# Value weights of a banded attention kernel: 16 contiguous elements a head, or 128 columns that stand 16 elements apart

## What is computed

```python
x = x + attention(layernorm(x), Wq, Wk, Wv, Wo)   # 16 heads of 16, a window of 64 keys back
x = x + ffn(layernorm(x), W1, b1, W2, b2)         # 1024 wide, relu, W1 and W2 rounded to -1, 0, 1
```

## Time and profile before

| | |
|---|---|
| time, median of 3 runs | 694.15 us (693.81 to 694.34) |
| profiled execution, its span | 690.4 us |
| profiled execution, its own time | not listed apart; the median is 3.75 us over the span |
| PE busy | 649.0 us, 94% of the span |
| DVE busy | 628.3 us, 91% |
| ACT busy | 623.9 us, 90% |
| POOL busy | 618.0 us, 90% |
| DMA packets | 497988 for 61.17 MB |

### The profile page before, as it was taken

How to read it: one execution, slowest core, us unless ns; L and a number is a source line. 1 busy time by engine, 2 the same in 40 slices (tenths; PEclk the granted TensorE clock), 3 DMA queues, 4 the chain that set the end, 5 groups by cost and what they waited for, 6 DMA issues and landing times.

```text
span 690.4 us, 24485 instructions
## 1 busy us (share of the span) xinstructions
PE 649.0 (94%) x8048; PEld 552.7 (80%) x8048; DVE 628.3 (91%) x1596; ACT 623.9 (90%) x2649; POOL 618.0 (90%) x869
## 2 busy tenths in 40 slices
PE   7668699999999999999999999999999999998887
PEld 5446488888888888888888888887888888887776
DVE  5779889999999999999999999999999999899864
ACT  5689899999999999999999999998999999898833
POOL 7388999999999999999999999999899999999930
PEclk9879989999999999999999999999999999999999
DMA  8576656465756656475756657475665646464000
GB/s 293 80 98 103 75 96 73 77 86 74 125 73 99 98 99 95 77 95 72 128 68 101 96 92 105 51 117 74 102 91 99 74 82 71 61 93 70 18 31 31
DMA packets 497988, 61.17 MB, mean 89 GB/s; under 512 B 470724, under 2 KB 493510, under 8 KB 497864
## 3 DMA queue, kind: packets, MB, share of 16 engines
q1 hardware_dynamic: 487160, 50.82, 51.2%
q10 hardware_dynamic: 10704, 8.80, 4.2%
HBM read 11.86 MB, written 8.39 MB: 29 GB/s over the span
## 4 chain that ended last, share of the span: by engine, by line
PE 40%; POOL 32%; issue 10%; ACT 9%; DVE 6%; DMA 1%; SPq 0%; POOLq 0%; DVEq 0%; ACTq 0%
POOL p L393 13%; POOL tl L417 10%; PE ps L1089 9%; PE ps L1077 7%; ACT p L496 6%; PE ps L987 5%; POOL th L411 5%; PE ps L967 5%; PE ps L1024 4%; PE ps L1035 3%; PE ps L1050 3%; ACT hTh L573 1%; PE ps L1062 1%; POOL rstdC L386 1%; PE ps L960 1%
## 5 line engine op out<-in xcount | busy, mean ns | idle before, releaser
L496 ACT ACTIVATE p<-ps,negm 128x96 f32<-128x96 f32 x1024 | 340.3, 375 | 8.4 <-DVE negm L711 7.7
L417 POOL TENSOR_TENSOR tl<-pt,th 128x384 f16<-128x384 f32 x256 | 234.6, 916 | 16.3 <-ACT th L505 1.8
L496 ACT ACTIVATION_READ_ACCUMULATOR p<-ps,negm 128x1 f32 x1024 | 248.5, 244 | 0.0
L393 POOL TENSOR_TENSOR p<-p,rden 128x384 f32<-128x384 f32 x256 | 214.3, 837 | 7.3 <-DVE rden L718 6.9
L724 DVE STREAM_TRANSPOSE pt<-p 128x384 f32<-128x384 f32 x256 | 141.5, 553 | 14.3 <-POOL p L393 12.9
L711 DVE TENSOR_REDUCE negm<-ps 128x4 f32<-128x384 f32 x256 | 136.0, 531 | 10.4 <-PE ps L967 8.1
L967 PE MATMUL ps<-k,qbd 128*128 128x96 f16 x1536 | 125.2, 208 | 0.0
L967 PEld LDWEIGHTS ps<-k,qbd 128*128 128x128 f16 x1536 | 106.0, 99 | 9.6
L987 PE MATMUL ps<-th,vb 128*128 128x96 f16 (+1 forms) x1120 | 97.1, 202 | 1.8 <-POOL tl L417 1.8
L1077 PE MATMUL ps<-xTCh,w1T 128*128 128x256 f16 x512 | 97.6, 272 | 0.8 <-ACT xTCh L568 0.8
L573 ACT ACTIVATE hTh<-ps 128x512 f16<-128x512 f32 x128 | 79.6, 623 | 19.9 <-PE ps L1077 19.7
(11 more groups left out here) (139 smaller groups left out, 1486.7 us busy)
## 6 DMA issues: line engine op xcount, KB each, us to landing
k<-kst SPq DMA_DIRECT2D x32, 288.0 KB, 4.1
vb<-vd SPq DMA_DIRECT2D x256, 32.0 KB, 2.6
out<-x SPq DMA_DIRECT2D x32, 256.0 KB, 2.5
qbd<-qs SPq DMA_DIRECT2D x254, 32.0 KB, 2.3
x<-in_L_attn_hidden ACTq DMA_DIRECT2D x15, 512.0 KB, 5.4
kw<-kst SPq DMA_DIRECT2D x31, 192.0 KB, 3.8
k<-kst SPq DMA_DIRECT2D x31, 144.0 KB, 3.4
vb<-in_L_ffn_W SPq DMA_DIRECT2D x2, 1024.0 KB, 7.6
```

The costliest lines, as they stand in the source:

```text
L393: e.tensor_tensor(p3, p3, rden[n % 4][:, :].unsqueeze(2).to_broadcast([128, 4, 96]), ALU.mult).then_inc(s_nm, 1)
L417: e.tensor_tensor(tl[g % 2][:, o], pt[n % 3][:, :], th[g % 2][:, o], ALU.subtract).then_inc(s_lo, 1)
L496: ins = e.activation(p[:, 96 * u:96 * u + 96], bank[:, 96 * u:96 * u + 96], ACT.Exp, bias=m[:, u:u + 1], accum_out=r[:, u:u + 1])
```

## The change

`vd` and `vb` get another order of dims. The innermost two are now t and g, and d stands outside them: `vd` is `[128, v 2, h 4, d 16, t 4, g 4]`, and `vb` has one more dim for m ahead of v. So for one head and one part v the values (d t g) are one run of 256 elements, 512 bytes, and a DMA of `place_v` moves two runs a partition where it moved 32. The weight columns (v h d) of a key block now stand 16 elements (32 bytes) apart. ACT and DVE write `vd` through the new order: 8 rows of 64 elements as before, but the 64 stand 16 elements apart, and DVE reads the high half with that step too. The sizes of the buffers, the bytes, the counts of instructions on all engines, their order and their semaphores are the same.

```diff
-        vd = sb("vd", [128, 4, 4, 2, 4, 16], f16)
-        vb = [sb(f"vb{i}", [128, 4, 4, 4, 2, 4, 16], f16) for i in range(3)]
+        vd = sb("vd", [128, 2, 4, 16, 4, 4], f16)
+        vb = [sb(f"vb{i}", [128, 4, 2, 4, 16, 4, 4], f16) for i in range(3)]
...
-                    src = vd[32 * m:32 * m + 32, :, :, :, h, :].rearrange("p t g v d -> p (t g v) d")
-                    dst = vb[b][32 * h:32 * h + 32, m, :, :, :, h, :].rearrange("p t g v d -> p (t g v) d")
+                    src = vd[32 * m:32 * m + 32, :, h].rearrange("p v d t g -> p v (d t g)")
+                    dst = vb[b][32 * h:32 * h + 32, m, :, h].rearrange("p v d t g -> p v (d t g)")
...
-                e.activation(vd[:, 2 * u:2 * u + 2, :, 0].rearrange("p t g h d -> p (t g) (h d)"),
+                e.activation(vd[:, 0, :, :, 2 * u:2 * u + 2, :].rearrange("p h d t g -> p (t g) (h d)"),
...
-                hi, lo = (vd[:, 2 * u:2 * u + 2, :, v].rearrange("p t g h d -> p (t g) (h d)") for v in range(2))
+                hi, lo = (vd[:, v, :, :, 2 * u:2 * u + 2, :].rearrange("p h d t g -> p (t g) (h d)") for v in range(2))
...
-                    lhs = vb[(c if k >= 0 else c - 1) % 3][:, k % 4, k % 16 // 4, g].rearrange("p v h d -> p (v h d)")
+                    lhs = vb[(c if k >= 0 else c - 1) % 3][:, k % 4, :, :, :, k % 16 // 4, g].rearrange("p v h d -> p (v h d)")
```

## The result

The changed kernel takes 768.67 us (median; 767.07 to 768.79) against 694.25 us: a ratio of 1.1059, with a 95% interval of 1.1041 to 1.1077. That is 74.4 us slower, outside the range of 692 to 750.

The account below looks back on a forecast made before the run. PE and POOL were taken to bound the kernel in turns, with four engines nearly full. Span 690.4 + 0 (DMAs) + 0 (loads) + 1.3 (writes) = 691.7 us, plus 3.75 to the median, 695.4 us; range 692 to 750.

Parts of the forecast that it names:

- PE and POOL in turns, four engines nearly full: Whole kernel: the chain is PE for 40% and POOL for 32%; PE, DVE, ACT, POOL busy 373.2 to 385.7 of 390 us.
- Nearly in full: PE, idle 4.3 us in ten chunks: whatever makes its stream longer is paid nearly in full.
- The value 0: Value DMAs: some 246 thousand fewer packets buy 0 us, at most the chain's 1% for DMAs, 6.9 us.
- The rival that named the first `values` group: Value DMAs: at most the first `values` gain from the relief, 1 to 3 us, 691 to 693 us; chance 4%.
- No wait of ours ends there: Value DMAs: next chunk's scores and `values` come later than SP's 14.04 us of issuing, so no wait ends on them.
- The 3.75 us that the sum adds to the span: The sum: the median stood 3.75 us above the profiled span, added to 691.7 us to give 695.4 us.
- I take a load that at most doubles and stays under its matmul: Weight loads of line 987: the stepped load stays hidden behind the 96-column matmul's 42 ns, at a price of 0.
- The first rival: Line 987: a load that shows, 53 to 70 ns; at 57 ns 39.9 us more on PE, 730 us; chance 22%.
- The estimate of 10 to 27 ns: Line 987: streaming time estimated for a contiguous float16 load of 128 columns, before the change.
- I bound it by 0 and by a doubling: Writes of vd: ACT's copy and DVE's low half at most double, 16.0 us on ACT and 19.2 on DVE.
- one of two ways to be wrong: Signs: line 987's 96-column matmul starts over 45 ns apart, or a step in the copies costing more than a doubling.
- the part that is paid I take as the share of the path: Writes of vd: 9% of ACT's 16.0 us and 6% of DVE's 19.2, 2.6 us if both double; middle 1.3 taken.

## Why the prediction was wrong

**What bounds the kernel.** PE and POOL in turns, four engines nearly full: right, and it fits that each of the three prices was mostly paid. "Nearly in full" for PE was too much: 37 of 50 us, 75%.

**The value DMAs.** The packets were right. The value 0 was off by 2 us. The rival that named the first `values` group, 1 to 3 us, had the size, and by the packets above the place. "No wait of ours ends there" was read from the waits that the profile puts down to a DMA; this one stood under POOL's name. That the gain of 2 us comes from this start alone isn't shown: the group starts 2 to 3 us earlier, but single profiles of these kernels have spans of 689.8 and 691.7 us against 690.4, so they scatter as much as the gain. The 3.75 us that the sum adds to the span are such scatter in part: in every run that lists both, the time stands 1.9 us over the span.

**The weight loads.** The step that failed is "I take a load that at most doubles and stays under its matmul". The load measured a pace of 61.5 ns, past the cover of 42; the price on PE is 50 us, and by itself 37.4. The first rival had it, with 53 to 70 ns, 40 us on PE at its middle and 730 us; loads alone took 731.8. That the two agree so closely is luck: the price on PE was 10 us more than at its 57 ns, and the absorbed part 8 or 9 us more than its 4, which was PE's idle time of ten chunks and not of sixteen. Nor did the load come to stream "about as long as a float32 one": it is listed with 161 ns, the float32 one with 141. The estimate of 10 to 27 ns (its lower end has no row behind it) for the contiguous load was not contradicted, but it said nothing of what limits a load whose columns lie apart: at steps of 8 and more the load's pace is at least 2.2 times the most that was estimated for the contiguous one. The fast load of 128 weights that the Trainium skill's page "TensorE: Matmul & The Clock Gate" (section "Weight-path perf modes") has for steps up to 1,024 elements may be in force here or not, which no run shows; the load slows all the same. The rule of its page "SBUF — State Buffer" (section "Door 1: The DMA port swizzle"), lines of 16 bytes, fits the flat part: little changes between 8 elements and 16 (158 and 161 ns). It has a step of 8 bf16 as still free, and here 4 already shows (115 ns for 98) and 8 costs nearly all of it; the measurement decides.

**The writes of vd.** This is the larger error. "I bound it by 0 and by a doubling": the copies quadruple on ACT, 0.50 to 2.01 us, and more than triple on DVE, 0.60 to 2.01. I had named this as one of two ways to be wrong. The Trainium skill's figure for a stepped destination (page "Vector Engine (DVE) Microarchitecture Reference", section "Measured stream behaviour on trn2") is 2.50 ns a column for 32-bit elements 24 words apart; here, with float16 elements 32 bytes apart, it is 2.01 us / 512 = 3.9 ns. Its estimate in the prediction, 0.74 us more for 0.60, already stood above the doubling that the sum took as its bound. And the second step failed too, "the part that is paid I take as the share of the path": ACT's share was 9%, while 32.4 of 48 us, 67%, was paid on ACT and 32.3 of 45, 72%, on DVE. A share of the chain says where the path ran, not what one more microsecond would do to an engine that is 97% busy. The idle time in the windows was the better measure, 12.5 and 13.2 us in ten chunks: an instruction of 2 us twice a chunk uses it up and pays the rest. By it (20 and 21 us in sixteen chunks, 1.6 times that in ten) and the real sizes, the writes come out at (48 - 20) + (45 - 21) = 52 us, where 68 was measured, or some 56 without the estimated 12 us of the low clock. That the two come so near may be chance: one engine at a time, the rule gives 28 and 24 us where 32.4 and 32.3 were measured.

**The rivals together.** They were taken one at a time, and the case that came was two at once, load and writes, which none of them held.

## What to carry to other kernels

A stepped operand is paid per instruction that touches it, so ask of each reader and writer how many adjacent elements it takes at a stretch, and in which order: the same layout cost 768.7 or 729.5 us by the order in which two instructions walked it. A weight load may grow until it reaches the pace of its matmul, here 42 ns for 96 columns, which a step of 4 keeps and a step of 8 does not. Where four engines are each nearly full, count a longer instruction against that engine's idle time, not against its share of the chain, and don't add the prices of several engines: 37 and 68 us made 74. Look at the granted clock of an experiment before taking its price: one that leaves PE waiting can bring the clock down and so cost more than the change it stands for, here an estimated 12 of 68 us. And check a wait against the program: the wait of 1.9 us for the value DMAs was listed under another engine.

## What the runs showed of the hardware

A float16 load of 128 columns goes from a pace of at most 29 ns at steps 1 to 3 to 37, 39, 47 and 60 ns at steps 4, 5, 6 and 8, and is 62 at 16. A copy of 512 float32 from PSUM to float16 in SBUF took ACT 0.48, 0.60, 1.09, 2.01 and 1.97 us at steps of 1, 2, 4, 8 and 16 elements, while reading PSUM 64 elements apart cost nothing when the writes came in runs of 8. Runs of 4 elements (8 bytes), with PSUM read 128 elements apart, were as fast (0.48 us on ACT, 0.60 on DVE). For DVE a stepped write (2.00 us) cost far more than a stepped second input (1.02 us), and both together no more than the write. In the kernel with stepped writes alone, PE's wait for DVE (2.3 us before 287.5 us) was followed by 3.4 us at a granted clock of 0.50, in which six matmuls of 512 columns took 2.59 us, where they take 1.47 us at 1.00.
